# The scan's products within a chunk, each issued as two products of 64 tokens in the two column groups of the TensorE array

## The chip, the cores and the metric

One core of one Trainium2 chip runs the whole program. The metric is the device time in microseconds (us); lower is better. The engines are named as in the profile: PE is TensorE (PEld is its loading of stationary operands), DVE is VectorE, ACT is ScalarE, POOL is GpSimd, and SP issues most of the DMAs.

## The reference, cut to what matters

Two transformer-like layers run one after the other on x of shape (2, 2048, 256): windowed attention and a soft mixture of experts, then a Mamba-2 state space block and a top-k mixture of experts. The change lies in the state space block, which the reference writes as a scan over tokens:

```python
dtx = dt[..., None] * xs                       # (B, L, 8 heads, 64)
def step(h, inp):
    dec_t, dtx_t, B_t, C_t = inp
    h = dec_t[:, :, None, None] * h + dtx_t[..., None] * B_t[:, None, None, :]
    y = jnp.einsum('bhpn,bn->bhp', h, C_t)
    return (h, y)
y = jnp.moveaxis(ys, 0, 1)
y = y + D_skip[None, None, :, None] * xs
y = y.reshape(B, L, INNER) * jax.nn.silu(z)
return y @ W_out + b_out
```

There are 8 heads of 64 features (INNER = 512) and a state of 64. The result must be float32.

## The kernel before

`state_space` works in chunks of 128 tokens: 16 chunks of each of 2 sequences, so 32 jobs, n = 0 to 31, alternating between the sequences. One job turns the scan over its 128 tokens into matrix products. The state carried in gives `pi` (`states(n)`, first product). What the chunk's tokens give to each other is, for each head, a product of a 128 by 128 matrix (source token by target token, the decayed and masked products of B and C, in `mt`, tile g_dlm) with `dtx` (128 source tokens by 64 features, tile g_wide). `within(n)` issues these 8 products, one for each head, in plain float32. The stationary operand is `mt[:, h, :]`, 128 columns wide; the moving operand is the head's 64 columns of `dtx`. All heads write into one PSUM bank, `py`: 128 tokens by 512 features. One semaphore, `y_ready`, is raised by the last of them.

The order on every engine is written out by hand. In round n, the tensor engine's queue holds: the input projection of job n+1 (`project`, 18 products at lines 69 to 71), `logits(n-4)`, `turn_y(n-1)` (4 transposes), `states(n)` (L2757 and L2764), `state_rows(n+1)` (2 transposes, L2731), `within(n)` (L2773), `turn_rows(n-3)` (2 transposes, L2790; from round 3 on), `correlate(n+1)` (L2741), and `outputs(n-1)` (12 products at lines 61 to 63). In every second round `by_expert` adds one transpose (L2808). `within(n)` waits for DVE's `weigh(n)`, which makes `mt` (L2478), for POOL's `dtx` (L2194) and for DVE having read `py` in the round before. DVE's `sums(n)` (L2519) reads `py` and is the reader that waits for `y_ready`; the next `weigh` and POOL's next `products` wait for it too.

A float32 product of the program stands in the trace as two pairs of a weight load and a matmul, so the 8 products of a job are 16 rows on PE and 16 on PEld, and the 256 products of the 32 jobs are 512 of each. The shape that the trace prints for a load, such as 128*128 or 128*64, is rows by columns of the array that are used.

Of the kernel before, what the change touches and what calls it, by code (L numbers as in the profile page):

```python
# [12 lines left out]
P = 128  # L13
# [859 lines left out]
HD = INNER // HEADS  # L873
# [1248 lines left out]
def state_space(nc, m, w):  # L2122


    with ExitStack() as ctx:
# [10 lines left out]
        xs, dtx, xw, xD, zr, y = [wide6[:, k] for k in range(6)]  # L2136
        m.hid_at = nc.sbuf_base - 3 * B * INNER * 4
        m.shared_hid = nc.alloc_sbuf_tensor_at("i_hid", [P, B, FT, GW], F32, offset=m.hid_at)
        le, mt = m.dlm[:, 0:B], m.dlm[:, B]
# [6 lines left out]
        py, pi, pst, pyT = [ps("g_p" + n, [P, 512]) for n in ("y", "i", "st", "yT")]  # L2146
# [567 lines left out]
        def _(pe):  # L2714
# [51 lines left out]
            def within(n):  # L2766
                b = n % B
                pe.wait_ge(s["m_done"], n + 1)
                pe.wait_ge(s["dtx_done"], n + 1)
                pe.wait_ge(s["t2_done"], n)  # L2770
                pe.wait_ge(s["ex_done"], max(n - 3, 0))
                for h in range(HEADS):
                    last = nc.tensor.matmul(py[:, h * HD:(h + 1) * HD], mt[:, h, :], dtx[:, b, h * HD:(h + 1) * HD],  # L2773
                                            start=True, stop=True)
                last.then_inc(s["y_ready"], 1)

            def outputs(n):
# [61 lines left out]
            for n in range(LAST):  # L2839
                if is_job(n + 1):  # L2840
                    project(n + 1)
                if is_job(n - 4):
                    logits(n - 4)
                if NJ <= n < NJ + 4:
                    first_up((n - NJ) // 2, (n - NJ) % 2)
                if is_job(n - 1):
                    turn_y(n - 1)
                if is_job(n):
                    states(n)
                if n == 3:  # L2850
                    late_turn()
                if is_job(n + 1):
                    state_rows(n + 1)
                if is_job(n):
                    within(n)
                if is_job(n - 3):
                    turn_rows(n - 3)
                if is_job(n + 1):
                    correlate(n + 1)
                if n == 2:  # L2860
                    late_cumulate()
                if is_job(n - 1):
                    outputs(n - 1)
                if n % B == 0 and is_job(n - 5):
                    by_expert((n - 6) // B)
# [758 lines left out]
```

## Time and profile before

| | |
|---|---|
| device time, median of 3 runs | 1643.37 us (1641.85 to 1644.45) |
| the profiled execution: span of its trace | 1640.7 us |
| what lies around the span, median less span | 2.7 us |
| PE busy, whole span | 1565.0 us, 95% |
| PEld, DVE, ACT, POOL busy | 83%, 73%, 48%, 35% |
| the state space jobs: first and last `within` | 858.9 us to 1166.5 us |

The table is read in this way: the engine with the highest share bounds the kernel only if it does so in the stage in question, so the stage is looked at by itself below. No time of the profiled execution is given other than its span. A change read from the trace is added to the span, and the 2.7 us around it are added again for the forecast of the median.

### The profile page before, as it was taken

What the parts mean: (1) busy time and instruction counts of PE and PEld (TensorE: products, weight loads), DVE (VectorE), ACT (ScalarE), POOL (GpSimd) and SP (SyncE); (2) the same over time, 40 slices, a digit from 0 to 9 for tenths busy, and PEclk for the clock granted to TensorE, in tenths of its full rate; (3) what the DMA queues carried; (4) which work ended last, traced back from release to release, by engine and by line L of the source; (5) the groups of instructions that cost most, each with busy time, mean ns of one, the idle gap of its engine ahead of it and who ended that gap; (6) DMA issues with size and microseconds to landing.
All of it is one profiled execution on the core that took longest, in us unless ns stands there. A gap on an engine that the chain in (4) does not pass through costs nothing. (4 is left out here: it accounts for less than half of the span.)

```text
span 1640.7 us, 25927 instructions
## 1 busy us (share of the span) xinstructions
PE 1565.0 (95%) x9320; PEld 1359.8 (83%) x9320; DVE 1202.6 (73%) x2680; ACT 787.8 (48%) x1578; POOL 578.1 (35%) x474
## 2 busy tenths in 40 slices
PE   6999989999999999999988999999799999999997
PEld 4689878988989888867877889888688788898896
DVE  6776688876668657655988899999778747666763
ACT  3333333455467245427257787778411325444442
POOL 2100020000000012320536878777300034777764
PEclk9999999999999999999989999999999999999999
DMA  7000000000020000212134223322232135665653
GB/s 237 5 1 1 1 1 27 1 27 1 1 103 27 14 5 16 94 58 85 34 106 158 80 81 92 89 81 81 77 133 63 39 100 152 159 160 137 162 108 39
DMA packets 81174, 116.35 MB, mean 71 GB/s; under 512 B 15724, under 2 KB 60312, under 8 KB 80152
## 3 DMA queue, kind: packets, MB, share of 16 engines
q1 hardware_dynamic: 67096, 96.21, 18.2%
q0 software_dynamic: 12288, 17.31, 5.9%
q8 instruction: 75, 1.23, 0.3%
q10 hardware_dynamic: 1664, 1.18, 0.2%
q14 instruction: 51, 0.42, 0.1%
HBM read 86.37 MB, written 27.68 MB: 70 GB/s over the span
## 5 line engine op out<-in xcount | busy, mean ns | idle before, releaser
L2120 POOL DMA_INDIRECT k_xe<-rows_dram,idx x64 | 82.5, 1289 | 174.7 <-DVE idx L3463 140.5
L2899 POOL DMA_INDIRECT out<-k_eo,idx x64 | 117.0, 1828 | 73.1 <-DVE k_eo L2993 58.8
L1948 PE MATMUL d_pO<-d_sp,d_raw 128*128 128x257 f32 x512 | 114.6, 380 | 3.3 <-DVE x L1330 3.2
L1948 PEld LDWEIGHTS d_pO<-d_sp,d_raw 128*128 128x128 f32 x512 | 95.6, 189 | 17.7 <-DVE x L1330 4.1
L583 ACT ACTIVATE b_p<-b_pS,b_nmax 128x384 f32<-128x384 f32 (+16 forms) x32 | 38.1, 1192 | 128.2 <-DVE b_nmax L725 128.2
L61 PE MATMUL b_pO<-b_vh,b_ph 128*128 128x256 f32 x302 | 87.7, 291 | 5.1 <-DVE b_pl L706 5.1
L63 PE MATMUL b_pO<-b_vl,b_ph 128*128 128x256 f32 x302 | 85.3, 283 | 0.0
L62 PE MATMUL b_pO<-b_vh,b_pl 128*128 128x256 f32 x302 | 85.3, 282 | 0.0
L373 POOL TENSOR_TENSOR x<-x,b_vrow 128x256 f32<-128x256 f32 x32 | 24.4, 792 | 163.3 <-DVE b_hs L652 163.2
L2354 ACT ACTIVATE g_dlm<-d_cumb,mod 128x128 f32<-128x128 f32 x256 | 78.6, 400 | 0.7 <-DMA d_cumb<-cum_dram 0.7
L2953 ACT ACTIVATE k_act_g<-i_pg 128x512 f32<-128x512 f32 x64 | 38.3, 598 | 83.5 <-PE i_pu L63 83.2
L61 PE MATMUL i_po<-k_wh,k_hh 128*128 128x256 f32 x256 | 72.6, 284 | 1.0 <-issue 0.6
L3219 ACT ACTIVATE i_act_g<-i_pg 128x512 f32<-128x512 f32 x30 | 17.9, 598 | 114.0 <-PE i_pu L63 111.9
L63 PE MATMUL i_po<-k_wl,k_hh 128*128 128x256 f32 x256 | 72.5, 283 | 0.0
L62 PE MATMUL i_po<-k_wh,k_hl 128*128 128x256 f32 x256 | 72.4, 283 | 0.0
L3010 DVE TENSOR_TENSOR k_hid<-k_act_g,i_pu 128x512 f32<-128x512 f32 x64 | 44.0, 688 | 38.1 <-ACT k_act_g L2953 37.6
L61 PE MATMUL b_pS<-b_kh,b_qh 128*128 128x512 f32 (+5 forms) x172 | 65.5, 381 | 1.4 <-DVE b_vl L698 1.4
L706 DVE TENSOR_TENSOR b_pl<-b_pT,b_ph 128x512 fp32r<-128x512 f32 (+3 forms) x86 | 49.7, 618 | 22.5 <-ACT b_ph L573 22.4
L69 PE MATMUL pL<-d_winh,g_uh 128*128 128x384 f32 x186 | 64.4, 346 | 0.8 <-ACT pL L2330 0.8
L2773 PE MATMUL g_py<-g_wide,g_dlm 128*128 128x64 f32 x512 | 61.4, 273 | 3.7 <-DVE g_dlm L2478 1.9
L2773 PEld LDWEIGHTS g_py<-g_wide,g_dlm 128*128 128x128 f32 x512 | 59.7, 192 | 5.9 <-issue 3.6
L61 PEld LDWEIGHTS b_pO<-b_vh,b_ph 128*128 128x128 f32 x302 | 57.6, 191 | 8.0 <-DVE b_pl L706 7.6
(590 smaller groups left out, 5450.1 us busy)
## 6 DMA issues: line engine op xcount, KB each, us to landing
d_cumb<-cum_dram SPq DMA_DIRECT2D x32, 512.0 KB, 4.2
k_wf<-in_WgT SPq DMA_DIRECT2D x16, 512.0 KB
k_wf<-in_WuT SPq DMA_DIRECT2D x16, 512.0 KB
k_wf<-in_WdT SPq DMA_DIRECT2D x16, 512.0 KB
rows_dram<-h_hx SPq DMA_DIRECT2D x32, 136.0 KB, 3.8
x<-in_x SPq DMA_DIRECT2D x8, 512.0 KB, 9.8
d_w<-in_w SPq DMA_DIRECT2D x4, 1024.0 KB, 6.2
uT_dram<-d_ug SPq DMA_DIRECT2D x16, 256.0 KB, 2.4
```

Source lines behind the costliest of these rows:

```text
L61: nc.tensor.matmul(out, ah, bh, start=start, stop=False)
L62: nc.tensor.matmul(out, al, bh, start=False, stop=False)
L63: return nc.tensor.matmul(out, ah, bl, start=False, stop=stop)
L69: nc.tensor.matmul(out, ah, bh, start=False, stop=False, skip_group_check=True)
L706: nc.vector.tensor_tensor(pl[:, r, 0:w], src[:, 0:w], ph[:, r, 0:w].bitcast(F32), ALU.subtract).then_inc(s["lo_done"], 1)
L1948: last = nc.tensor.matmul(pO[:, t % 2, 0:PW], raw[e][:, t * P:(t + 1) * P], proc[e], start=e == 0, stop=e == E - 1)
L2120: nc.gpsimd.indirect_dma_start(out=m.xe[:, e % 2, t, :], out_offset=None, in_=m.rows, in_offset=bass.IndirectOffsetOnAxis(ap=column(m, e, ...
L2354: nc.scalar.activation(le[:, b, h, :], cumb[:, b, h, :], ACT.Relu, bias=cs[:, b, 3, h:h + 1], scale=-1.0).then_inc(s["dd_done"], 1)
L2773: last = nc.tensor.matmul(py[:, h * HD:(h + 1) * HD], mt[:, h, :], dtx[:, b, h * HD:(h + 1) * HD], start=True, stop=True)
L2899: nc.gpsimd.indirect_dma_start(out=out, out_offset=bass.IndirectOffsetOnAxis(ap=column(m, e, t), axis=0), in_=eo[:, e % 2, t, :], in_offse ...
L2953: nc.scalar.activation(act_g[:, f % 2], pg[:, f % 2], ACT.Gelu).then_inc(s["gelu_done"], 1)
L3010: nc.vector.tensor_tensor(hid[:, f % 2], act_g[:, f % 2], pu[:, f % 2], ALU.mult).then_inc(s["hid_done"], 1)
```

## The change

The loop over heads gets an inner loop over two halves of the 128 target tokens. Each half is a product of its own: its stationary operand is 64 columns of `mt`, its moving operand is the same 64 columns of `dtx` as before, and its result goes to 64 partitions of `py`. The result's partitions decide which columns of the array a product uses: the first half uses columns 0 to 63, the second half columns 64 to 127. The program marks all of these products with an array tile of 128 rows by 64 columns, at column 0 or column 64; those around them are marked 128 by 128. The semaphore is still raised by the last product.

```diff
                 for h in range(HEADS):
-                    last = nc.tensor.matmul(py[:, h * HD:(h + 1) * HD], mt[:, h, :], dtx[:, b, h * HD:(h + 1) * HD],
-                                            start=True, stop=True)
+                    for rows in (slice(0, P // 2), slice(P // 2, P)):
+                        last = nc.tensor.matmul(py[rows, h * HD:(h + 1) * HD], mt[:, h, rows], dtx[:, b, h * HD:(h + 1) * HD],
+                                                start=True, stop=True)
                 last.then_inc(s["y_ready"], 1)
```

On PE, in the first jobs (rounds without `turn_rows`), the queue changes as follows. g_py is `py`, g_wide is the storage of `dtx`, g_dlm that of `mt`, and pL holds the transposes and the correlation.

```order
 L2764 MATMUL g_pst<-g_wide,mod 128x512
 L2731 MATMUL pL<-ident,mod 128x128 x2
-L2773 MATMUL g_py<-g_wide,g_dlm 128x64 x8
+L2774 MATMUL g_py<-g_wide,g_dlm 64x64 x16
 L2741 MATMUL pL<-g_bcT 128x128
 L69 MATMUL pL<-d_winh,g_uh 128x384
```

Eight products of 128 by 64 become sixteen of 64 by 64, between the same neighbours.

On PE, in a later round, where `turn_rows` follows, the piece before is this one (L2800 is `logits`, L2747 `turn_y`):

```order
L2800 MATMUL g_py<-h_mgw,uT 128x16 x2
L2747 MATMUL g_pyT<-ident,g_wide 128x128 x4
L2757 MATMUL g_pi<-g_H,g_bcT 128x512
L2764 MATMUL g_pst<-g_wide,mod 128x512
L2731 MATMUL pL<-ident,mod 128x128 x2
L2773 MATMUL g_py<-g_wide,g_dlm 128x64 x8
L2790 MATMUL g_pi<-ident,h_hx 128x128 x2
L2741 MATMUL pL<-g_bcT 128x128
L61 MATMUL g_pyT<-d_wogh,g_yh 128x256
```

After the change it reads:

```order
L2801 MATMUL g_py<-h_mgw,uT 128x16 x2
L2747 MATMUL g_pyT<-ident,g_wide 128x128 x4
L2757 MATMUL g_pi<-g_H,g_bcT 128x512
L2764 MATMUL g_pst<-g_wide,mod 128x512
L2731 MATMUL pL<-ident,mod 128x128 x2
L2774 MATMUL g_py<-g_wide,g_dlm 64x64 x16
L2791 MATMUL g_pi<-ident,h_hx 128x128 x2
L2741 MATMUL pL<-g_bcT 128x128
L61 MATMUL g_pyT<-d_wogh,g_yh 128x256
```

Nothing moved past anything else; the lines behind the change are numbered one higher. On the other engines and in the DMA queues no instruction is added or moved.

## Rows read from the trace of the kernel before

**Rows 1.** The page, busy time of each engine over the span.

```profile
PE 1565.0 (95%) x9320; PEld 1359.8 (83%) x9320; DVE 1202.6 (73%) x2680; ACT 787.8 (48%) x1578; POOL 578.1 (35%) x474
```

**Rows 2.** Busy time by stretch: the first four jobs, then the 26 jobs after them.

```profile
core 0: us, PE busy (x) PEld busy (x) DVE busy (x) ACT busy (x) POOL busy (x), PEclk, DMA share, GB/s
858.94:902.79 43.85, 38.90 (x235) 33.26 (x234) 38.39 (x73) 32.39 (x83) 29.25 (x26) 0.96 0.46 158
902.79:1155.89 253.10, 250.58 (x1679) 222.25 (x1678) 227.69 (x490) 201.28 (x573) 200.61 (x158) 1.00 0.29 85
```

**Rows 3.** Busy time by stretch: two rounds, each from one `within` to the next.

```profile
1000.06:1009.67 9.61, 9.61 (x67) 8.60 (x66) 8.99 (x21) 7.53 (x22) 7.42 (x7) 1.00 0.31 88
1009.67:1019.18 9.51, 9.51 (x67) 8.51 (x65) 8.28 (x18) 7.84 (x23) 8.00 (x7) 1.00 0.29 86
```

**Rows 4.** Timeline of PE around `within(14)`: start us, us, instruction, count.

```profile
999.84 0.38 PE L2731 MATMUL pL<-ident,mod 128*128 128x128 f32 x2
1000.06 1.90 PE L2773 MATMUL g_py<-g_wide,g_dlm 128*128 128x64 f32 x16
1001.79 0.39 PE L2790 MATMUL g_pi<-ident,h_hx 128*128 128x128 f32 x2
```

**Rows 5.** Timeline of the weight loads there: start us, us, instruction, count.

```profile
999.95 1.87 PEld L2773 LDWEIGHTS g_py<-g_wide,g_dlm 128*128 128x128 f32 x16
1001.68 0.26 PEld L2790 LDWEIGHTS g_pi<-ident,h_hx 128*128 128x128 f32 x2
```

**Rows 6.** Line L2773: durations ns min/median/max, first and last start; idle before it.

```profile
L2773 PE MATMUL g_py<-g_wide,g_dlm x512: 222/275/324, 858.9 to 1166.5; 128*128 128x64 f32 x171
  DVE g_dlm L2478: 4.1, 2
  issue: 3.6, 6
```

**Rows 7.** Timeline of the matmuls around L1978, a product on 64 columns.

```profile
778.55 0.28 PE L1977 MATMUL pL<-d_f_dA,d_after 128*128 128x128 f32 x1
778.76 0.32 PE L1978 MATMUL pL<-d_f_dA,d_ones 128*64 128x128 f32 x1
...
778.92 0.27 PE L1978 MATMUL pL<-d_f_dA,d_ones 128*64 128x128 f32 x1
779.12 0.48 PE L1948 MATMUL d_pO<-d_sp,d_raw 128*128 128x257 f32 x1
```

**Rows 8.** Timeline of the weight loads there.

```profile
778.75 0.13 PEld L1978 LDWEIGHTS pL<-d_f_dA,d_ones 128*64 128x64 f32 x1
...
778.81 0.14 PEld L1978 LDWEIGHTS pL<-d_f_dA,d_ones 128*64 128x64 f32 x1
...
779.12 0.30 PEld L1948 LDWEIGHTS d_pO<-d_sp,d_raw 128*128 128x128 f32 x2 [0.17 <-DVE x L1330]
```

**Rows 9.** Timeline around L2815, another product on 64 columns.

```profile
885.42 0.28 PE L2814 MATMUL g_pst<-g_fdA,d_after 128*128 128x112 f32 x1
885.62 0.31 PE L2815 MATMUL g_pst<-g_fdA,d_ones 128*64 128x112 f32 x1
...
885.77 0.26 PE L2815 MATMUL g_pst<-g_fdA,d_ones 128*64 128x112 f32 x1
885.96 0.39 PE L61 MATMUL g_pyT<-d_wogh,g_yh 128*128 128x256 f32 x1
```

**Rows 10.** Timeline around L3295, a transpose on 64 array rows.

```profile
1325.87 0.27 PE L3295 MATMUL j_pI<-ident,k_area 64*128 64x64 f32 x1
1326.08 0.70 PE L3320 MATMUL i_po<-ws_d,i_hid 128*128 128x256 f32 x2
```

**Rows 11.** Timeline of DVE in the round of rows 4.

```profile
1002.87 0.68 DVE L2519 TENSOR_TENSOR g_wide<-g_py,g_wide 128x512 f32<-128x512 f32 x1
...
1005.11 1.22 DVE L2478 TENSOR_TENSOR g_dlm<-g_dlm,mod 128x1024 f32<-128x1024 f32 x1
```

## The prediction

> **What bounds the kernel now.** I read the page first: PE is busy 95% of the span and its weight loads 83%, DVE 73% [rows 1]. That says nothing yet about the state space jobs, so I cut the span there. In the first four jobs PE has 38.90 of 43.85 us and DVE 38.39, so neither is full. In the 26 jobs behind them PE has 250.58 of 253.10 us, or 99%, DVE 90%, at a granted clock of 1.00, which is the 2.4 GHz level [rows 2]. Two single rounds say the same: 9.61 and 9.51 us long, PE busy for all of it, DVE for 8.99 and 8.28 [rows 3]. So what `within` gains or loses on PE is gained or lost in the round, and a gain can go on only until DVE fills.
>
> Next, what `within` costs. The 16 matmuls begin at 1000.06, and what is behind them begins at 1001.79: 1.73 us, or 0.108 a pair [rows 4]. What sets that pace? The weight loads reach from 999.95 to L2790's at 1001.68, with 16 starts in 1.73 us [rows 5]. Inside the series it is (1.87 - 0.19) / 15 = 0.112 from one start to the next. A matmul streams only 64 columns. L1978's two matmuls stream 128 columns behind short loads: the first streams when its load is in, at 778.81, and the second starts at 778.92 [rows 7, 8], so 128 columns stream in about 0.107 and 64 in 0.053. The load of 128 columns therefore sets the pace, and half of the array's streaming time is unused. Over the 32 jobs the two largest idle times in front of these products, 4.1 and 3.6 us, come to 7.7 us [rows 6].
>
> **The change part by part.** It takes out 16 pairs a job and puts in 32, each with a load of 64 columns.
>
> *The pace inside.* Two loads of 64 columns start 0.055 apart (778.75 and 778.81) [rows 8]. 32 x 0.055 = 1.76 us, against 16 x 0.112 = 1.79. If the 0.112 is 0.107 of loading, as much as streaming 128 columns, and a fixed 5 ns, half the columns take 0.058, and 32 take 1.86. So the inside costs -0.03 to +0.07; I take +0.03. It can't be much less unless the two halves of the array work at once, which is a rival below. The reason that I don't take that: the order is load, matmul, load, matmul, and a float32 product is two such pairs on the same columns. In the rows above each load starts when the matmul in front has begun, and never two loads ahead. Of four pairs (A1, A2 on the first half, B1, B2 on the second), A2 must wait for A1's stream, B1's load stands behind A2, and B2 waits for B1's stream. Worked out with 0.053 for each load and stream, a round of four still takes 4 x 0.054.
>
> *Going in.* Around L1978 the array changes from 128 to 64 columns. The matmul in front starts at 778.55; the load of the next would start with it, but starts at 778.75, 0.20 later, and its matmul streams only after the load, at about 778.81 [rows 7, 8]. L2815 shows the same: 885.42, then 885.62 [rows 9]. In front of `within` stand transposes of 128 columns, normally 0.11 ahead of it (the second at 999.95) [rows 4, 5]. With the change the first stream begins 0.20 + 0.055 = 0.255 behind it: +0.15 a job.
>
> *Coming out.* The last matmul of L1978 starts at 778.92, the load behind it at 779.12: 0.20, of which 0.107 is streaming, so about 0.095 is emptying the array [rows 7, 8]. The other case gives 0.19 with 112 columns, 0.093 + 0.095 [rows 9]. For 64 columns that is 0.053 + 0.095 = 0.148. Then the load behind is no longer hidden: 0.107 where it is L2741's (L1948's matmul lasts 0.48 with its load in it [rows 7]), about 0.053 where it is a transpose's (L3295 to L3320 is 0.20: load 0.053, stream 0.053, emptying 0.095) [rows 10]. So 0.20 in most jobs, against about 0.06 now (load and matmul of L2790 follow with one stream between them): +0.14 a job.
>
> The Trainium skill (TensorEngine Tiling (Array Packing), Key Properties) says that changing the tiling mode, not just the tile, drains the engine. The trace agrees, at 0.20 us where 0.11 is usual [rows 7]. By that rule going from the first half to the second costs nothing, and there are two changes a job; without it there would be up to 17, the last rival.
>
> *Sum.* 0.03 + 0.15 + 0.14 = 0.32 us a job; with the ends of the pace, and 0.05 more where L2741 stands behind, 0.26 to 0.41. A round's other work isn't late: DVE reads `py` at 1002.87, 0.9 after the last product's end (1000.06 + 1.90) [rows 4, 11], and `weigh` for the next job is done at 1006.33, over 3 us before it is used. `correlate` and `outputs` stand behind `within` on PE and slip with it, and DVE's 8.99 fit well into 9.9 [rows 3]. So the round grows by the sum in the 26 jobs that PE fills. In the first four others set the pace, and some of PE's 7.7 us of waiting will take up part [rows 2, 6]; I count 28 jobs: 28 x 0.32 = 9.0 us. The profiled span of 1640.7 becomes 1649.7, and with the 2.7 around it the median 1643.4 becomes 1652.4. The ends: 24 x 0.26 = 6.2 and 32 x 0.41 = 13, so 1650 to 1656.5; with the spread of the runs, 1649 to 1658.
>
> **The rivals.** 0.2% (3.3 us) is about what a measurement can tell from no change.
>
> *Both halves work at once (faster).* If a load for the second half is taken ahead of a waiting matmul of the first, two pairs fit into 0.055 us. Inside then 31 x 0.028 = 0.87, in all 0.255 + 0.87 + 0.20 = 1.32 from the transpose to what follows, against 1.85 now (999.95 to about 1001.80). That is -0.53 a job. DVE's 8.99 with its small gaps leave about 0.4 of that [rows 3]: 28 x 0.4 = 11 us less, 1632 (1627 to 1638). It decides from a pace below 0.045 a pair, where it has paid for the two changes. For it: the paths of the halves are separate in result and weights. Against it: the alternating loads and matmuls above, and no row has work in the second half. Chance 0.22.
>
> The Trainium skill (TensorE: Matmul & The Clock Gate, Part 3) says that products in different column groups run concurrently, and gives 2.38 times the speed for three tiles of 32 columns; it also says that loads are pulled ahead of matmuls in flight. No row of this case shows either.
>
> *The two cancel (same).* A partial overlap at 0.042 to 0.048 a pair gives 0.455 + 31 x 0.045 = 1.85, what it is now: 1643 to within 3 us. Chance 0.06.
>
> *Many more instructions, or every half empties the array (much slower).* No row shows pairs going at 0.055 for long; the longest series in these rows go at 0.108. If the queue gives out a pair each 0.09, a job costs 0.455 + 31 x 0.09 - 1.85 = +1.4, 32 x 1.4 = 45 us: 1688. If each of the 15 further steps from half to half empties the array, they cost 0.148 + 0.053 - 0.055 = 0.146 each, 2.2 a job, 70 us: 1714. In between, 0.062 a pair gives +0.53 and 1658. For it: nothing in the rows excludes it. Against it: a round's 67 pairs are handed out without a gap on PE [rows 3]. Chance 0.12 for above 1659, all together.
>
> *My forecast.* Chance 0.60.
>
> **How the numbers follow.** The likeliest gives 1652.4, its own range is 1649 to 1658. Leaving it at that would leave out 0.4, so the range goes down to take most of the faster case: 1630 to 1659 leaves out the much slower case and the lowest part of the faster one, 0.12 + 0.05. Faster by over 0.2%: 0.22 + 0.02 = 0.24. Within 0.2%: 0.06. Slower: 0.60 - 0.02 + 0.12 = 0.70.
>
> **What would show it.** In the timeline, the first load of `within` 0.20 behind the second transpose's start and not with it; the loads of 64 columns 0.055 apart in a steady row, on both halves alike; L2791's load 0.15 behind the last matmul; from `within` to what follows 2.0 us and not 1.73; rounds of 9.85 to 9.95 where now 9.51 and 9.61; DVE's share of the round down to about 88%. It is wrong if matmuls on the second half start with those on the first (two in 0.055), or if gaps of 0.1 or more stand between the halves. The clock should stay at 1.00, since streaming and loading fill most of each round.

## The result: faster by 0.6%, where slower was forecast

| | before | after |
|---|---|---|
| device time, median | 1643.74 us (1641.85 to 1644.45, 4 runs) | 1634.68 us (1633.1 to 1637.15, 4 runs) |
| span of the profiled execution | 1640.7 us | 1631.4 us |

The ratio is 0.9944, 95% interval 0.993 to 0.9958. The likeliest time of the forecast was 1652.4, slower than before; 1634.68 lies in the stated range of 1630 to 1659, near the rival in which both halves of the array work at once, on the side that had the smaller chance.

The page of the changed kernel, engines over the span; PE and PEld each have 512 instructions more, as the change says [rows 1].

```profile
PE 1551.0 (95%) x9832; PEld 1338.3 (82%) x9832; DVE 1193.1 (73%) x2680; ACT 784.8 (48%) x1578; POOL 576.6 (35%) x474
```

Busy time by stretch, the same jobs as in [rows 2], then two rounds, as in [rows 3]:

```profile
core 0: us, PE busy (x) PEld busy (x) DVE busy (x) ACT busy (x) POOL busy (x), PEclk, DMA share, GB/s
860.79:903.49 42.70, 36.88 (x299) 29.72 (x298) 37.94 (x73) 32.45 (x83) 28.47 (x26) 0.96 0.47 162
903.49:1145.49 242.00, 237.30 (x2094) 203.06 (x2093) 217.72 (x490) 198.39 (x573) 200.16 (x158) 1.00 0.30 89
...
1005.69:1014.70 9.01, 9.01 (x81) 7.77 (x80) 8.02 (x19) 7.74 (x23) 7.57 (x7) 1.00 0.34 90
1014.70:1023.84 9.14, 9.14 (x82) 7.90 (x81) 8.31 (x20) 7.39 (x23) 7.57 (x7) 1.00 0.31 91
```

The 26 rounds take 242.00 us where they took 253.10, 0.43 less a round, and the first four 42.70 where they took 43.85. A round that PE fills, as these two, is about 0.50 us shorter, with PE still busy throughout.

The timeline of PE and of the weight loads around `within(15)`, which answers to [rows 4, 5]:

```profile
1005.38 0.38 PE L2731 MATMUL pL<-ident,mod 128*128 128x128 f32 x2
1005.70 1.15 PE L2774 MATMUL g_py<-g_wide,g_dlm 128*64 128x64 f32 x32
1006.78 0.44 PE L2791 MATMUL g_pi<-ident,h_hx 128*128 128x128 f32 x2
1007.05 0.39 PE L2741 MATMUL pL<-g_bcT 128*128 128x128 f32 x2
...
1005.38 0.14 PEld L2731 LDWEIGHTS pL<-ident,mod 128*128 128x128 f32 x1 [0.29 <-issue]
1005.69 1.01 PEld L2774 LDWEIGHTS g_py<-g_wide,g_dlm 128*64 128x64 f32 x32 [0.17 <-issue]
1006.77 0.20 PEld L2791 LDWEIGHTS g_pi<-ident,h_hx 128*128 128x128 f32 x2
```

All 32 matmuls run within 1.15 us. They last 0.222 us each (the median of the line), so from the first start to the last it is 1.15 - 0.22 = 0.93 us: 31 steps of 0.030. With every load and every stream of 64 columns taking over 0.05, that can't be done one after the other. The start itself shows it. Here are the first loads of that job, in a window of 4 ns:

```profile
1005.69 0.14 PEld L2774 LDWEIGHTS g_py<-g_wide,g_dlm 128*64 128x64 f32 x2 [0.17 <-issue]
```

Two loads of 0.13 us lie within 0.14 us: the second began under 10 ns behind the first, where two loads into the same 64 columns stood 0.055 apart [rows 8].

The change of tile size is there as forecast. The second transpose starts at 1005.49 and the first load at 1005.69, 0.20 behind it, the "0.17 <-issue" of the row. At the end 1006.78 - (1005.70 + 0.93) = 0.15. The two matmuls of L2791 then last 0.44 us and not 0.39 [rows 4]: the first has its own load in it, which was hidden before. So what a job gains is read one step further on, at `correlate` (L2741). In the kernel before it stands here, beside [rows 4]:

```profile
1002.02 0.39 PE L2741 MATMUL pL<-g_bcT 128*128 128x128 f32 x2
```

From the first transpose to `correlate` it was 1002.02 - 999.84 = 2.18 us and is 1007.05 - 1005.38 = 1.67: 0.51 less, as the rounds say.

**The whole span.** In these two profiles the scan rounds give 11.10 + 1.15 = 12.25 us less, the span only 9.3. The rest lies in two places outside, where no instruction was changed, and where the granted clock was lower. The first two rows are of the changed kernel; the last is of the kernel before:

```profile
470.00:475.00 5.00, 3.64 (x16) 2.95 (x15) 3.57 (x5) 2.19 (x2) 0.00 (x0) 0.73 0.00 0
...
1170.00:1175.00 5.00, 3.74 (x16) 2.42 (x14) 1.27 (x6) 2.92 (x7) 0.00 (x0) 0.80 0.25 85
```

```profile
470.00:475.00 5.00, 3.64 (x21) 3.15 (x21) 3.81 (x5) 3.07 (x4) 0.00 (x0) 1.00 0.00 0
```

At 470 us PE was at 0.73 of its clock for 5 us, so for about half of them at 1.2 GHz, where it had 1.00 before; it did 16 matmuls and not 21. The first scan job starts 1.85 us later (860.79 for 858.94). After the scan there is such a stretch again. PE has gaps in both stretches, but at 470 us it had as many in the kernel before, so why the clock fell in one execution and not in the other stays open. The 1.15 us of the first four jobs can't be put down to the change either. These are the same jobs in the second profile of the changed kernel:

```profile
860.75:906.29 45.54, 38.00 (x299) 31.53 (x298) 38.45 (x73) 32.40 (x83) 28.65 (x26) 0.93 0.46 153
```

They take 45.54 us at a granted clock of 0.93, more than before the change. That profile has a span of 1634.9 us, 3.5 more, with the same 26 rounds (241.8), so this much changes from run to run. What is the change's own is the 11 us of the 26 rounds.

### The profile page after: what moved, and what is told of

Same layout as the page of the kernel before. It is cut to its first block and busy times, and to the rows that moved or that the text cites. A ratio compares the mean times of both kernels' runs of the same rounds, so it can differ in the third digit from the quotient of the medians.

```text
span 1631.4 us, 26951 instructions
## 1 busy us (share of the span) xinstructions
PE 1551.0 (95%) x9832; PEld 1338.3 (82%) x9832; DVE 1193.1 (73%) x2680; ACT 784.8 (48%) x1578; POOL 576.6 (35%) x474
## 5 line engine op out<-in xcount | busy, mean ns | idle before, releaser
L1674 ACT COPY d_raw<-pL 128x512 f32<-128x512 f32 x64 | 37.4, 587 | 55.9 <-PE pL L63 55.9
```

## The experiments

Eight kernels were run, each beside the kernel before on the same chip; its median was 1643.76 us beside run2, run8, one_group and two_heads, and 1643.04 beside the other four. "Inside" is from the first matmul of `within` to the last, in the rounds that PE fills.

| kernel | inside, us | round, us | median, us | ratio, 95% interval |
|---|---|---|---|---|
| before | 1.62 | 9.51, 9.61 | 1643.74 | |
| the change, repeated | 0.93 | 9.01, 9.14 | 1631.4 | 0.9916 (0.9889 to 0.9943) |
| run2 | 0.98 | 9.05, 9.19 | 1634.45 | 0.9938 (0.9915 to 0.996) |
| run4 | 1.32 | 9.39, 9.54 | 1639.66 | 0.9978 (0.9964 to 0.9992) |
| run8 | 1.68 | 9.75, 9.89 | 1645.53 | 1.0011 (1.0002 to 1.0021) |
| one_group | 1.86 | 9.93, 10.07 | 1653.78 | 1.0057 (1.0037 to 1.0077) |
| two_heads | 1.66 | 9.63, 9.75 | 1646.05 | 1.001 (0.9997 to 1.0023) |
| quarters | 0.88 | 8.95, 9.06 | 1632.23 | 0.9924 (0.9898 to 0.995) |
| states_too | 0.93 | 8.77, 9.26 | 1632.96 | 0.9936 (0.9912 to 0.9961) |

### one_group: is it two halves at once?

```diff
-                        last = nc.tensor.matmul(py[rows, h * HD:(h + 1) * HD], mt[:, h, rows], dtx[:, b, h * HD:(h + 1) * HD],
+                        out = rows if n == 0 else slice(0, P // 2)
+                        last = nc.tensor.matmul(py[out, h * HD:(h + 1) * HD], mt[:, h, rows], dtx[:, b, h * HD:(h + 1) * HD],
```

> As the changed kernel, but from the second job on both halves of the tokens are computed on array columns 0 to 63 and written to the first 64 rows of the result, the second over the first, so the values of the chunk's inner product are not those of the reference; the number, the shapes and the order of the products are as in the change. This is the forecast's own case: no two halves at once, and two changes of the tile size a job. By the forecast's sum: pairs at 0.055 to 0.058, 1.76 to 1.86 us, from the second transpose to what follows 2.1 to 2.25 us against 1.84 before, rounds of 9.85 to 9.95, and 1650 to 1656. If a single half also went faster than 0.055 a pair, the gain of the change would not come from two halves at once: 1635.

The timeline of PE in job 14, its weight loads, and the two rounds behind it:

```profile
1004.74 0.38 PE L2731 MATMUL pL<-ident,mod 128*128 128x128 f32 x2
1005.05 2.08 PE L2775 MATMUL g_py<-g_wide,g_dlm 128*64 128x64 f32 x32
1007.34 0.39 PE L2741 MATMUL pL<-g_bcT 128*128 128x128 f32 x2
...
1005.05 1.94 PEld L2775 LDWEIGHTS g_py<-g_wide,g_dlm 128*64 128x64 f32 x32 [0.17 <-issue]
...
1005.05:1015.12 10.07, 10.07 (x82) 8.83 (x82) 9.00 (x21) 7.65 (x22) 7.44 (x7) 1.00 0.29 84
1015.12:1025.05 9.93, 9.93 (x82) 8.69 (x81) 8.28 (x18) 7.71 (x23) 7.99 (x7) 1.00 0.24 82
```

2.08 - 0.22 = 1.86 us for 31 steps: 0.060 a pair. The first step is longer than the others; from load to load it is (1.94 - 0.14) / 31 = 0.058. The same products in the same number, all on one half, take twice the 0.93 us, and the kernel is slower than before, by 10 us. So the gain is that of two halves at once. That this run writes one result over the other is not what slows it: run8, below, goes at the same pace on one half (six matmuls in its first 0.35 us) and writes nothing over. This run is also the forecast's case on the chip: 1653.8 for 1652.4.

### two_heads: what do the two changes of tile size cost?

```diff
-                    for rows in (slice(0, P // 2), slice(P // 2, P)):
+                    for rows in ((slice(0, P // 2), slice(P // 2, P)) if h < 2 else (slice(0, P),)):
```

> Heads 0 and 1 as in the change (8 pairs of 64 columns), heads 2 to 7 as before (12 pairs of 128 columns). The two changes of tile size are still paid, the gain only for two heads. Worked out from the profiles: a head costs 2 x 0.112 before and 2 x 0.058 now, 0.107 less; all eight give 0.86 less, and the measured gain of a job from the second transpose to what follows is 0.557, so the two changes cost 0.30. Two heads then give -0.21 + 0.30 = +0.09 us a job, rounds of about 9.6 to 9.7, and 1644 to 1648: no faster than before the change, or a little slower. If the changes of tile size cost nothing, it would be 1638 to 1640.

```profile
1012.60 0.38 PE L2731 MATMUL pL<-ident,mod 128*128 128x128 f32 x2
1012.91 1.93 PE L2774 MATMUL g_py<-g_wide,g_dlm 128*64 128x64 f32 x20
1014.68 0.39 PE L2791 MATMUL g_pi<-ident,h_hx 128*128 128x128 f32 x2
1014.90 0.28 PE L2741 MATMUL pL<-g_bcT 128*128 128x128 f32 x1
...
1012.91:1022.54 9.63, 9.63 (x69) 8.39 (x69) 8.28 (x18) 7.72 (x23) 7.99 (x7) 1.00 0.30 86
```

From the transposes to what follows it is 14.68 - 12.60 = 2.08 us, against 1.95 before [rows 4]: +0.13, where +0.09 was expected. The rounds are 0.12 longer, and the time can't be told from before. Two heads don't pay for the two changes. By +0.13 = cost - 2 x 0.107, the changes cost about 0.34 us a job. All eight heads give 0.86 less by their pace, and `correlate` comes 0.51 earlier, so it is 0.35 there. (The 0.30 in the text above takes 0.557, read at L2791's start; that leaves out the 0.05 us of its load, which is no longer hidden.) One_group agrees: `correlate` comes 1007.34 - 1004.74 = 2.60 us behind the first transpose, 0.42 later than before, of which the pace inside is about 0.07. At 0.107 a head it takes more than three heads to break even.

### run2, run8, run4: how far ahead does a half take its products?

The edit, for run2; run8 and run4 have 8 and 4 in the place of 2:

```diff
-                for h in range(HEADS):
+                for h0 in range(0, HEADS, 2):
                     for rows in (slice(0, P // 2), slice(P // 2, P)):
+                        for h in range(h0, h0 + 2):
```

> The changed kernel with another order: two heads on the first half of the array, then the same two on the second half, and so on; the same products and the same result. Theory A (each half takes its products from the common queue by itself, ahead of products that wait for the other half): the place in the order matters little, the 32 pairs of a job still take 0.93 us from first to last start, and the kernel stays at 1634 to 1637. Theory B (only neighbours in the order overlap, so the gain of the change hangs on strict alternation): of four pairs in a row on one half three go one by one at 0.055, so a job's pairs take 1.4 to 1.75 us, and the kernel comes to 1645 to 1653.

> As run2, with all eight heads on the first half (16 pairs), then all eight on the second. Theory A with a queue that reaches 32 instructions ahead: 0.93 us again, 1634 to 1637. Theory A with a short reach: the first half works alone until its last pairs, about 16 x 0.058 + 16 x 0.058 = 1.8 us, and the kernel comes to about 1651. Theory B: the same 1.8 us. So this run tells the reach, together with run2.

Run2 has four pairs in a row on one half, and inside it takes 0.98 us, so strict alternation isn't what the gain hangs on: the other half's work was taken ahead of pairs that had to wait. Run8 lies between what was written for a long reach and for a short one. How many matmuls and loads it has under way in fifths of its job 14, and then from the start of the job up to two moments 0.02 us apart:

```profile
core 0: us, PE busy (x) PEld busy (x), PEclk, DMA share, GB/s
999.70:1000.05 0.35, 0.35 (x6) 0.35 (x7) 1.00 0.00 0
1000.05:1000.40 0.35, 0.35 (x10) 0.35 (x9) 1.00 0.00 0
1000.40:1000.75 0.35, 0.35 (x13) 0.35 (x12) 1.00 0.00 0
1000.75:1001.10 0.35, 0.35 (x12) 0.35 (x9) 1.00 0.00 0
1001.10:1001.45 0.35, 0.35 (x9) 0.35 (x7) 1.00 0.00 0
...
999.70:1000.44 0.74, 0.74 (x12) 0.74 (x13) 1.00 0.00 0
999.70:1000.46 0.76, 0.76 (x14) 0.76 (x15) 1.00 0.00 0
```

The counts take in what is still running from the fifth before. They rise around the one place where the first half's series ends and the second's begins, and nowhere else. Up to 0.74 us twelve matmuls have started, one after the other; then two start within 0.02 us of each other. If the products are given out in the order of the program, the fourteenth is the second half's first, and three of the first half's 16 still wait at that time. Against one_group's 1.86 us, run8 saves 0.18: three pairs of 0.060 are hidden at that seam. From this the next run was worked out before it ran:

> Four heads on the first half, the same four on the second, then the other four in the same way: runs of 8 pairs on one half. The traces of the runs of 4 pairs and of 16 pairs suggest that a half takes its next product from the queue when at most about three pairs of the other half stand in front of it. Then each of the three seams between runs hides three pairs of 0.058: 32 x 0.058 - 3 x 3 x 0.058 = 1.33 us from first to last start, rounds of about 9.4, and 1639 to 1642. If the reach is longer than a run of 8 pairs, it is 0.95 and 1635; if only the seam of a single pair counts, 1.7 and 1647.

```profile
998.30 0.38 PE L2731 MATMUL pL<-ident,mod 128*128 128x128 f32 x2
998.61 1.54 PE L2775 MATMUL g_py<-g_wide,g_dlm 128*64 128x64 f32 x32
1000.09 0.44 PE L2792 MATMUL g_pi<-ident,h_hx 128*128 128x128 f32 x2
```

1.54 - 0.22 = 1.32 us, three seams of 0.18 less than 1.86. The rounds, 9.39 and 9.54, and the time, 1639.7, came as written. So a half gets its next product past about three waiting pairs of the other half, and no more. Two mechanisms would look like this, and no run tells them apart: one queue that looks ahead, or a short queue for each half, filled in the order of the program, which holds about three waiting pairs and stops the filling when it is full.

### quarters: does the load or the stream set the pace now?

```diff
-                    for rows in (slice(0, P // 2), slice(P // 2, P)):
+                    for rows in [slice(q * P // 4, (q + 1) * P // 4) for q in range(4)]:
```

> Four products of 32 tokens a head, in four column groups: 64 pairs of 32 columns a job. If a group's pace is set by streaming its 64 columns (0.053 and 5 ns), the four groups at once give 16 x 0.058 = 0.93 us as now, and the same time as the change, 1633 to 1637. If the load set the pace, 16 x 0.032 = 0.5 us, 1625. If the queue can't feed four groups (a pair each 0.0146), or its reach of about three pairs is too short for the two pairs of each of four groups, it is above 0.93: with two groups at a time 32 x 0.058 = 1.86 and about 1652.

```profile
1006.49 0.38 PE L2731 MATMUL pL<-ident,mod 128*128 128x128 f32 x2
1006.80 1.10 PE L2774 MATMUL g_py<-g_wide,g_dlm 128*32 128x64 f32 x64
1007.83 0.44 PE L2791 MATMUL g_pi<-ident,h_hx 128*128 128x128 f32 x2
```

64 pairs inside 1.10 - 0.22 = 0.88 us, one each 0.014, four groups at once. The loads are half as long and it gains only 0.05, so the stream of 64 columns sets the pace of a group (15 steps of 0.058 are 0.87). The time, 1632.2, is that of the change. The queue can give out a pair in 0.014 us for 64 pairs, which also ends the rival of too many instructions.

### states_too: can the rest of the stage use it?

```diff
+                    state_rows(n + 1)
                 pe.wait_ge(s["xw_done"], n + 1)
-                nc.tensor.matmul(pst[:], bc[:, b, 0, :], xw[:, b], start=True, stop=True).then_inc(s["st_ready"], 1)
+                nc.tensor.matmul(pst[0:STATE, 0:256], bc[:, b, 0, 0:STATE], xw[:, b, 0:256], start=True, stop=True)
+                nc.tensor.matmul(pst[STATE:P, 256:512], bc[:, b, 0, 0:STATE], xw[:, b, 256:512], start=True, stop=True).then_inc(s["st_ready"], 1)
...
-                nc.vector.tensor_tensor(H[0:STATE, b], H[0:STATE, b], pst[0:STATE, :], ALU.add).then_inc(s["h_done"], 1)
+                nc.vector.tensor_tensor(H[0:STATE, b, 0:256], H[0:STATE, b, 0:256], pst[0:STATE, 0:256], ALU.add)
+                nc.vector.tensor_tensor(H[0:STATE, b, 256:512], H[0:STATE, b, 256:512], pst[STATE:P, 256:512], ALU.add).then_inc(s["h_done"], 1)
```

> The changed kernel, and the product that makes the chunk's state (512 columns streamed twice, 0.86 us) split in the same way: heads 0 to 3 on the first half of the array, heads 4 to 7 on the second, 256 columns each, put directly in front of the heads' products so that no further change of tile size is paid; the two transposes go ahead of it. VectorE adds the two parts to the state in two instructions instead of one. If halves with longer streams work at once too, 0.43 us a job goes on TensorE; VectorE gets about 0.17 a job more, and was busy for 8.3 to 9.0 of 9.1, so it will take over as the bound: rounds of 8.8 to 8.9 and 1628 to 1632. If VectorE's two instructions cost as much as they save, 1635.

The timeline of PE, and the busy time over the scan:

```profile
1005.57 0.43 PE L2768 MATMUL g_pst<-g_wide,mod 128*64 128x256 f32 x1
1005.57 0.43 PE L2769 MATMUL g_pst<-g_wide,mod 128*64 128x256 f32 x1
1005.83 0.38 PE L2768 MATMUL g_pst<-g_wide,mod 128*64 128x256 f32 x1
1005.84 0.38 PE L2769 MATMUL g_pst<-g_wide,mod 128*64 128x256 f32 x1
1006.39 1.15 PE L2779 MATMUL g_py<-g_wide,g_dlm 128*64 128x64 f32 x32 [0.17 <-POOL g_wide L2194]
...
903.50:1145.50 242.00, 231.02 (x2149) 199.23 (x2149) 224.84 (x516) 198.07 (x578) 198.76 (x158) 1.00 0.32 91
```

Streams of 256 columns also start in twos, at 1005.57 and again at 1005.83. Here the two halves stand on two lines, so the trace itself says which is which, and it is the most direct sign of the whole case: L2769's first matmul starts before L2768's second, though L2768 stands first in the program. As far as the two pairs of a float32 product stand together in the queue, as they do elsewhere in the trace, the second half's work went past a waiting pair of the first. But PE now waits in front of the heads' products: over the 26 rounds 3.7 us for POOL's `dtx` and 4.5 us for ACT (L2370), where the change had 0.9 and 1.3. Over 242 us it is busy for 231.02 and not 237.30, and DVE for 224.84 and not 217.72. The rounds, 8.77 and 9.26 in turn, are 0.05 shorter on average than those of the change, and the time, 1633.0, is that of the change within the scatter of the runs. The expected 1628 to 1632 was a little too low: what PE gave up went mostly into these waits and not into the round. No version tried beats the change clear of the scatter.

### The change once more

> The change once more, unaltered, beside the others on one chip: 1633 to 1637. The stage of the scan should repeat to 0.5 us (rounds of 9.01 and 9.11 to 9.14), and what differs in the span should lie in stretches where the granted clock is below 1.00, at other places than in the first profile.

The inside is 0.93 us again and the rounds are 9.00 to 9.14. The median, 1631.4, was a little below what was written. This profile's span was 1634.9 us. Its first scan job starts where it did in the first profile (860.75 us for 860.79), but job 4 at 906.3 us and not at 903.5, which is the 45.54 us shown above, and the granted clock was 0.83 from 1150 to 1190 us, where the first profile had 0.91 and the kernel before 0.96.

## Why the prediction was wrong

**The step that failed** is "the pace inside": that of the pairs A1, A2, B1, B2 the load of B1 stands behind A2 and can't pass it, so that a round of four takes 4 x 0.054. It doesn't have to wait. In the change the first loads of the two halves start under 10 ns apart, and in states_too the second half's first matmul starts before the first half's second. Run2, run4 and run8 show that work for the other half gets past about three waiting pairs. A group of the change has only two pairs on one half, so both halves always have work, and a round of four takes 2 x 0.058 and not 4 x 0.054. That this is a reordering queue, and not a short queue for each half, is not shown.

The evidence behind that step did not bear on it. In the rows of the kernel before, no load starts two ahead, but there neighbouring products use the same columns, and one_group shows that such pairs go one by one in any case. Such rows can't tell a queue in strict order from one that looks ahead. The Trainium skill (TensorE: Matmul & The Clock Gate, Part 3), weighed as a rival, said that products in different column groups run concurrently; the runs agree, at 0.030 us a pair on two halves against 0.060 on one, with the first step counted in.

**What held.** The other terms came out nearly. Going in was 0.20 us, as forecast. Coming out was 0.15 for 0.148, and then 0.05 for the load that is no longer hidden, also as forecast. One half alone went at 0.058 a pair, the upper end of 0.055 to 0.058. But the sum for work on one half was +0.32 us a job, and one_group has +0.42, just beyond the 0.26 to 0.41 of the forecast: the pace inside costs about 0.07 for the 0.03 taken, and the two changes about 0.35 for 0.15 + 0.14. Its median, 1653.8, still lies near 1652.4, in part by luck, since not every round grew by the 0.42. Its 26 rounds took 8.7 us more than before (261.84 for 253.10, +0.34 on average), its first four none:

```profile
861.97:904.95 42.98, 39.30 (x299) 32.42 (x298) 37.96 (x73) 32.45 (x83) 28.48 (x26) 0.96 0.48 162
904.95:1166.79 261.84, 260.28 (x2094) 227.21 (x2093) 227.09 (x490) 201.13 (x573) 200.61 (x158) 1.00 0.29 82
```

That PE sets the pace of most rounds, and that the rest of the round only slips with `within`, held too.

**The rivals.** "Both halves work at once" gave 1.32 us from the transpose to what follows and 1632 us; the change has 0.20 + 0.93 + 0.15 + 0.05 = 1.33 and 1634.7, or 1631.4 in the second set. It took DVE to leave only 0.4 of the 0.53 us for 28 jobs, 11 us; the rounds that PE fills fell by 0.50, but the 26 rounds by 0.43 on average, 11.1 us, and the first four by nothing that repeats. "The two cancel" and "every half empties the array" are ruled out by the 0.93 us, and the feeding of the queue by quarters.

**The chances.** The faster case had 0.22. With nothing in the rows against it but an order that could not have looked otherwise, it deserved at least as much as the forecast.

## What to carry to other kernels

Small products whose weight loads set the pace, here with a moving operand of 64 columns, are worth splitting over column groups: a pair with 128 columns cost 0.112 us, its two halves at once 0.058. Entering and leaving the smaller tile size costs 0.34 to 0.35 us together, so it takes six to seven such pairs in a row to break even, and the series must not be broken by other products. Issue the groups in turns of one or two products; runs of eight pairs on one group left about a quarter of the gain (rounds of 9.39 us, for 9.51 before and 9.01 with the change), and runs of sixteen none. And evidence for an order must come from a place where another order was possible.

## What the runs showed of the hardware that was not expected

A group takes its work past about three waiting pairs of another (0.18 us hidden at each seam, in run8 and in run4 alike). Whether the limit is one of instructions, pairs or time was not tried. Where both groups stand on one line, as in `within`, the trace doesn't say on which of them an instruction ran, and this was read from paces and counts; in states_too, with a line for each, it does. TensorE gave out 64 pairs of load and matmul in 0.88 us, 7 ns an instruction. Two executions of the changed kernel differed by 3.5 us of span, a third of the change's gain. 2.8 of it lies in the first four scan jobs (granted clock 0.96 and 0.93), the rest behind the 26 rounds (0.91 and 0.83 from 1150 to 1190 us).
